# Paged attention: masked scores written in four runs by key number modulo four, new keys at the ends of the runs

## What is computed

```python
kc = k_cache[block_table].reshape(bsz, L, HK, D)      # L = 16 pages * 32 = 512 cached keys
vc = v_cache[block_table].reshape(bsz, L, HK, D)
k_all = jnp.concatenate([kc, k], axis=1)              # and 32 new keys: 544
v_all = jnp.concatenate([vc, v], axis=1)
valid_c = jnp.arange(L)[None, :] < cache_seqlens[:, None]
valid = jnp.concatenate([valid_c, jnp.ones((bsz, seqlen), dtype=bool)], axis=1)
scores = jnp.einsum('bqhd,bkhd->bhqk', q, k_all) * SCALE
scores = jnp.where(valid[:, None, None, :], scores, -1e+30)
probs = jax.nn.softmax(scores, axis=-1)
o = jnp.einsum('bhqk,bkhd->bqhd', probs, v_all)
```

## Time and profile before

| | |
|---|---|
| median of 3 runs | 1679.14 us (1677.95 to 1681.06) |
| the profiled execution's own time | 1680.12 us |
| its span, first to last instruction | 1678.3 us |
| PE busy | 1620.6 us (97%) |
| DVE busy | 1113.4 us (66%) |
| ACT busy | 943.5 us (56%) |
| POOL busy | 254.1 us (15%) |
| mean granted TensorE clock | 0.995 |

### The profile page before, as it was taken

One profiled execution on the slowest core, in us unless ns is written; L12 is line 12 of the kernel. 1 busy time (PEld: TensorE's weight loads), 2 busy tenths in 40 slices (PEclk: granted clock), 3 DMA queues, 4 the chain that ended last, 5 costly groups with the idle time before them and its releaser, 6 DMA issues. The chain is left out here.

```text
span 1678.3 us, 34056 instructions
## 1 busy us (share of the span) xinstructions
PE 1620.6 (97%) x10792; PEld 1417.5 (84%) x10792; DVE 1113.4 (66%) x2941; ACT 943.5 (56%) x2392; POOL 254.1 (15%) x274
## 2 busy tenths in 40 slices
PE   2899999999999999999979999999999999999998
PEld 2887888888888788888869999999999999977777
DVE  8405543454446757777768888888888888864443
ACT  3224323232332256667658999999899989822221
POOL 1000000000000146656520010001000100022210
PEclk9999999999999999999989999999999999999999
DMA  6621222201210333443568989998999899595401
GB/s 232 210 89 50 68 70 69 69 29 40 69 63 26 144 119 108 135 126 115 156 235 274 303 291 301 308 304 287 309 301 306 283 315 300 178 320 143 122 12 50
DMA packets 225487, 290.69 MB, mean 173 GB/s; under 512 B 17146, under 2 KB 181402, under 8 KB 221338
## 3 DMA queue, kind: packets, MB, share of 16 engines
q1 hardware_dynamic: 220826, 222.90, 42.1%
q0 software_dynamic: 4608, 67.11, 11.2%
HBM read 237.44 MB, written 50.41 MB: 172 GB/s over the span
## 5 line engine op out<-in xcount | busy, mean ns | idle before, releaser
L1602 PE MATMUL p_val<-probs_t,vals 128*128 128x128 f32 x2048 | 270.7, 275 | 1.7 <-DMA vals<-in_v_pages,rows_now 1.7
L1602 PEld LDWEIGHTS p_val<-probs_t,vals 128*128 128x128 f32 x2048 | 251.4, 193 | 1.9 <-DMA vals<-in_v_pages,rows_now 1.9
L1512 DVE CUSTOM_DVE_ANT_0 probs<-p_score,mask 128x544 f32<-128x544 f32 x256 | 184.4, 720 | 58.5 <-issue 48.1
L1417 ACT ACTIVATE probs<-probs,low 128x544 f32<-128x544 f32 x256 | 190.2, 743 | 0.3 <-DVE low L1512 0.3
L1581 PE MATMUL p_turn<-cst,probs 128*128 128x128 f32 x1024 | 167.1, 286 | 0.1
L1501 DVE TENSOR_TENSOR wo_lo<-keys,wo_hi 128x544 fp32r<-128x544 f32 x224 | 161.8, 722 | 0.7 <-ACT wo_hi L1412 0.7
L1425 ACT ACTIVATE probs_t<-p_turn 128x512 f32<-128x512 f32 x256 | 149.1, 582 | 20.9 <-PE p_turn L1581 20.9
L457 PE MATMUL p_tile<-w_hi,y_hi 128*128 128x512 f32 x384 | 156.7, 408 | 2.4 <-PEq L470 2.4
L1412 ACT ACTIVATE wo_hi<-keys 128x544 fp32r<-128x544 f32 x224 | 146.0, 652 | 20.3 <-PE p_score L459 18.6
L457 PE MATMUL p_score<-wo_hi,q_hi 128*128 128x288 f32 x448 | 149.9, 335 | 1.9 <-DVE low L1512 1.0
L459 PE MATMUL p_tile<-w_hi,y_lo 128*128 128x512 f32 x384 | 150.4, 392 | 0.0
(11 more groups left out here) (218 smaller groups left out, 3511.3 us busy)
## 6 DMA issues: line engine op xcount, KB each, us to landing
keys<-in_k_pages SPq DMA_DIRECT2D x512, 128.0 KB
qk_new<-x_res SPq DMA_DIRECT2D x80, 256.0 KB, 2.2
x_res<-qk_new SPq DMA_DIRECT2D x32, 512.0 KB
o_new<-x_res SPq DMA_DIRECT2D x32, 512.0 KB, 8.6
w_raw<-in_w_vkq_t SPq DMA_DIRECT2D x12, 1024.0 KB, 5.4
w_raw<-in_w_qkv_t SPq DMA_DIRECT2D x10, 1024.0 KB, 8.5
toep<-kpad SPq DMA_DIRECT2D x32, 256.0 KB, 4.4
w_raw<-in_w_dense_t SPq DMA_DIRECT2D x8, 1024.0 KB, 5.4
```

The lines of the kernel that those rows point to most:

```text
L1417: nc.scalar.activation(probs[:, i % 8, :], probs[:, i % 8, :], ACT.Exp, bias=low[:, i % 4:i % 4 + 1], scale=-1.0, accum_out=total[:, i % 4 ...
L1512: v.tensor_tensor_reduce(out=probs[:, i % 8, :], in0=score_at(i % 2, slice(0, KEYS)), in1=mask[:, i // HK, :], scale=1.0, scalar=3e38, op0 ...
L1602: mm = pe.matmul(p_val[:, h, half * P:(half + 1) * P], vals[:, slot, c // RUN, c % RUN * HK * D + k * D:c % RUN * HK * D + (k + 1) * D], p ...
```

## The change

Within a row of `probs` the order of the 544 keys changes. Before, key 4j+r stands at column 4j+r. Now it stands at column 136r+j: four runs of 136, run r with all keys whose number is r modulo 4. The 32 new keys (512 to 543) take the last 8 columns of each run.

```diff
+        by_run = lambda a: a.rearrange("p (r j) -> p j r", r=RUN)
+        in_order = lambda a: a.rearrange("p (j r) -> p j r", r=RUN)
+        chunk_at = lambda n: n % RUN * (KEYS // RUN) + n // RUN * P
...
-                    nc.scalar.activation(probs_n[:, q % 2, :, :], probs[:, q % 2 * NEW:(q % 2 + 1) * NEW, CACHE:KEYS],
+                    nc.scalar.activation(probs_n[:, q % 2, :, :].rearrange("p h (j r) -> p h j r", r=RUN),
+                                         probs[:, q % 2 * NEW:(q % 2 + 1) * NEW, :].rearrange("p h (r j) -> p h j r", r=RUN)[:, :, CACHE // RUN:, :],
                                          ACT.Copy).then_inc(new_gathered, 1)
...
-                v.tensor_tensor_reduce(out=probs[:, i % 8, :], in0=score_at(i % 2, slice(0, KEYS)), in1=mask[:, i // HK, :],
+                v.tensor_tensor_reduce(out=by_run(probs[:, i % 8, :]), in0=in_order(score_at(i % 2, slice(0, KEYS))), in1=in_order(mask[:, i // HK, :]),
                                        scale=1.0, scalar=3e38, op0=ALU.add, op1=ALU.min,
...
-                    mm = pe.transpose(p_turn[:, n, :], probs[:, i % 8, n // RUN * P * RUN + n % RUN:(n // RUN + 1) * P * RUN:RUN], ident)
+                    mm = pe.transpose(p_turn[:, n, :], probs[:, i % 8, chunk_at(n):chunk_at(n) + P], ident)
```

## The result

The changed kernel takes 1705.61 us (median of 4, 1703.62 to 1706.86) against 1680.1 us for the kernel before in the same comparison: a ratio of 1.0148, 95% interval 1.0136 to 1.016, or about +25 us. Forecast were 1696 us in a range of 1681 to 1720, so +17 us: right in sign and in which engine takes the lead, 8 us short in size. Further down it is shown that two terms of the sum were off in opposite directions.

The account below looks back on a forecast made before the run. PE bounds the kernel at 18.53 us a sequence. DVE then leads: 16.15 + 8 x 0.345 = 18.91, plus 0.15 of waiting, 19.06 us; 0.53 more over 32 sequences is +17 us, giving 1696 us, range 1681 to 1720.

Parts of the forecast that it names:

- PE leads before, DVE has 0.30 us to spare per masking: Kernel before: PE sets 18.53 us a sequence, DVE works 16.15, leaving 2.38 idle, 0.30 for each of 8 maskings.
- The stepped write costs 0.345 us an instruction, from L394: Masking on DVE: extra per instruction, the middle of 0.31 and 0.38 us read off L394, a similar stepped write.
- The lead changes to DVE and hides the transposes' 13.8 us: DVE needs 18.91 us a sequence, PE 18.10; plain transposes save PE 0.43 a sequence, 13.8 us over all, hidden under DVE.
- The gather on ACT is hidden: ACT's gather of new keys: 0.09 us more an instruction, 0.18 a sequence, costed at nothing; 6 us without cover.
- Hand-overs of 0.15 us a sequence: DVE's split waits for ACT's `split_hi`, queued behind `take_values`: some 0.12, say 0.15 us, once a sequence.
- the write did not hide: Rival: masking's write hides in DVE's slack, PE keeps the lead; extra below 0.24 us, full gain 13.8 us, 1665 us; chance 0.12.
- steep: Rival: masking's stepped write costs 0.76 us an instruction, a sequence 22.4 us, +123 us, 1802 us; chance 0.07.
- The two cancel: Rival: write extra of 0.27 to 0.31 us, no wait on ACT, sequence 18.3 to 18.6 us, within 0.2% of 1679; chance 0.10.
- What would show it: Profile signs: masking 1.03 to 1.10 us, transposes 272 ns, DVE near 490, PE idle before scores 0.8, masks 19.06 us apart.

Follow-up runs that it names:

- Run 1: The kernel before with only the transposes' reads made plain (128 neighbouring columns each), masking and gather as before: 1669.73 us against 1680.91, ratio 0.9939.
- Runs 7 and 8: The changed kernel with masking's write putting neighbours 32 floats apart, then 8, instead of 136: 1706.4 and 1714.19 us.
- run 2: The changed kernel with the transposes reading every fourth column again: 1707.51 us, ratio to the kernel before 1.0156.
- run 4: The changed kernel with ACT's gather of the new keys reading the last 32 columns of each head in order: 1707.71 us, ratio to the kernel before 1.0157.
- Run 3: The changed kernel with ACT's `take_values` put ahead of the exponent of the same step: 1699.44 us, ratio to the kernel before 1.0106.
- run 5: The kernel before with plain transposes, the splits writing runs of eight neighbours into the new order and masking writing plainly: 1677.27 us against 1680.5, ratio 0.9981.
- run 6: The changed kernel with masking's step moved from its write to its PSUM score reads, mask constants laid in run order: 1669.13 us against 1680.5, ratio 0.9937.

## Why the prediction was right, and what it missed, step by step

- *PE leads before, DVE has 0.30 us to spare per masking*: right on the lead. Run 1 shows it, 0.37 us a sequence gained (0.43 forecast) as soon as PE's own work shrinks. The spare time proved not usable to its end, see the hand-overs.
- *The stepped write costs 0.345 us an instruction, from L394*: right within about a tenth. Recorded it is +0.40 us (0.38 read off L394), the engine's own loss +0.31 (0.31 to 0.33 read off it). Both readings of L394 carried over, each to its own quantity; it was the start-to-start one that the sum needed. Runs 7 and 8 show why the row carried over: the step's size hardly matters. Taken at 0.31, this term is 2.48 us a sequence and not 2.76.
- *The lead changes to DVE and hides the transposes' 13.8 us*: right, shown by run 2.
- *The gather on ACT is hidden*: right, shown by run 4, though it grew by 0.12 us and not 0.09.
- *Hand-overs of 0.15 us a sequence*: this is the term that was mis-sized. It is 19.37 - 18.63 = 0.74 us. I had found `take_values` and the split's wait behind it, and put the wait at 0.12 to 0.15; the profile lists 0.17 as idle, but start to start the split loses 0.33. And I had followed `take_values` only to the split, not to its other reader: the value products of the next sequence wait until it has emptied the PSUM tile (15.5 us over the stage), and this makes scores and the next masking late. Run 3 removes that wait and gives back 0.24 us a sequence. With the measured values the sum is 16.15 + 2.48 + 0.74 = 19.37, which the 0.74 closes by its definition, and 0.84 x 32 = +27 us. The text allowed 0.4 us a sequence, 13 us, for rougher hand-overs; they took 0.59 more than assumed, 19 us. Of the 0.74 us, run 3 shows 0.24 as due to that order, and its timeline 0.27 more as the split's wait. Another 0.13 is the late first masking of a pass, which the forecast did not contain; some 0.1 us stays unattributed.
- *The nearness of the sum is partly luck*. The forecast's 0.53 us a sequence was 0.38 of DVE's own work over the old pace (12 us) and 0.15 of hand-overs (5 us). Measured are 18.63 - 18.53 = 0.10 (3 us) and 0.74 (24 us). The write was taken 9 us too dear in all and the hand-overs 19 us too cheap. DVE takes the lead, as forecast, but most of the loss is waiting that comes with it and not its own longer work.
- *The rivals*: the write did not hide (it would have had to cost under 0.24 us), and it was not steep. "The two cancel" was nearer than its chance of 0.10 says: the 0.31 us measured is the upper end of its condition, and only the waits kept it from coming true. Its "within 0.2%" was too narrow for its lower end, since 0.27 us gives 18.31 us a sequence, 7 us or 0.4% faster.
- *What would show it*: masking 1.12 us (1.03 to 1.10 expected), transposes 272 ns, DVE 483 of 500 us (near 490), masks 19.37 us apart (19.06). PE's wait ahead of the scores was far smaller than the 0.8 us a sequence forecast: the weight loads of L457 waited 9.6 us over the stage, 0.3 a sequence, and the products themselves 0.2 us in all. Most of PE's idle, 15.5 us, stood at the value products.

The Trainium skill's page Vector Engine (DVE) Microarchitecture Reference, section "Measured stream behaviour on trn2", fits this kernel in three points, though its hops are of 4 KiB and these are shorter: a hopping destination (estimate from its figure 0.36 us, measured 0.31 and 0.40), a hopping source (1.73 ns a column against 1.054, 0.68 more; here (1153 - 720) / 544 = 0.80 ns more a column), and free hops between runs of neighbours (run 5). Its 2.50 ns for a step of +24 words has no counterpart at 8, 32 or 136 floats here; at 8 the extra is 0.82 ns a column.

## What to carry to other kernels

Before moving a step from one engine's operand to another's, ask which engine has time to spare, and in what amount for each instruction: here PE's 0.05 us a head (four transposes of 0.0135) was bought with DVE's 0.31 us a masking, and DVE had 0.30. Spare time that is only just enough is not enough: DVE's own work came out 0.10 us a sequence over the old pace, and 0.74 us of waiting came with it. Then look for a place where the permutation is free: a read from PSUM that must happen anyway, or a constant that can be laid in the new order, gave the same layout and the full gain (run 6, ratio 0.9937). And when an engine takes the lead, follow every instruction queued behind its waiter to all of its readers, not only to the first.

## What the runs showed that I had not expected

- VectorE reads float32 from PSUM with a step of 4 floats (16 bytes) at the plain rate: 720 ns for 544 columns, as without a step. With the same step on the SBUF source as well, it takes 433 ns more.
- A stepped write and a stepped read are recorded as nearly equally long (1120 and 1153 ns), but the next instruction starts after 0.96 us in the one and 1.06 in the other, so recorded durations alone misprice them.
- A TensorE weight load with a step of 16 bytes is recorded at 210 ns and a plain one at 140, yet the pace of the transposes differs by only 0.0135 us each: most of that difference is covered.
